# Softmax of a gated attention layer on one core: eight of sixteen heads shifted and exponentiated by ScalarE instead of VectorE

## What is computed

```
q = LN(x) Wq + bq;  k = ctx Wk + bk;  v = ctx Wv + bv     (16 heads of width 64)
probs = softmax(q k^T / 8)                                (over the 64 context rows, for each head)
x = x + tanh(g_xattn) * (probs v Wo + bo)
x = x + tanh(g_ffn) * FFN(LN(x))        (a shared expert, and the best 2 of 8 experts for each token)
```

## Time and profile before

| | us |
|---|---|
| median of 3 runs | 307.4 |
| lowest and highest | 306.29, 309.32 |
| the profiled execution's own time | 309.48 |
| its span, first to last instruction | 307.7 |
| PE busy, share of the span | 278.0, 90% |
| DVE busy | 241.7, 79% |
| ACT busy | 163.9, 53% |
| POOL busy | 170.0, 55% |

### The profile page before, as it was taken

The page is one execution under the profiler, slowest core; times in us unless marked ns, Lnnn a source line. Parts: engine busy times, 40 slices in busy tenths (PEclk is TensorE's granted clock), DMA queues, the critical chain, the costliest instruction groups (busy, mean ns, idle before and its releaser), DMA issues.

```text
span 307.7 us, 6608 instructions
## 1 busy us (share of the span) xinstructions
PE 278.0 (90%) x1746; PEld 248.8 (81%) x1747; DVE 241.7 (79%) x687; ACT 163.9 (53%) x426; POOL 170.0 (55%) x236
## 2 busy tenths in 40 slices
PE   2999979999999899999986969987799999999992
PEld 1788757898897798999876948876799899999881
DVE  0489869999999699989999575778877777777755
ACT  1462785666756566673653434744355565657611
POOL 8012216787757876897886775409553444444520
PEclk9999999999999999999998897999999999999999
DMA  6999994133379999713031122313244434343697
GB/s 186 367 295 318 269 293 119 47 90 94 102 207 292 306 315 325 223 36 105 35 104 37 53 87 88 90 53 105 69 123 126 118 92 121 113 129 105 223 344 264
DMA packets 45006, 49.74 MB, mean 162 GB/s; under 512 B 3928, under 2 KB 41650, under 8 KB 44978
## 3 DMA queue, kind: packets, MB, share of 16 engines
q1 hardware_dynamic: 39938, 39.37, 44.4%
q0 software_dynamic: 3408, 8.46, 8.1%
q10 hardware_dynamic: 1632, 1.57, 1.5%
HBM read 21.67 MB, written 28.64 MB: 163 GB/s over the span
## 4 chain that ended last, share of the span: by engine, by line
PE 47%; DVE 26%; issue 9%; DMA 6%; ACT 6%; POOL 3%; SPq 1%; DVEq 0%; ACTq 0%; POOLq 0%
PE bank L1404 5%; PE bank L1406 4%; PE bank L1405 4%; PE scores_ps L1404 4%; DVE probs L1156 4%; PE scores_ps L1406 3%; DVE pT_lo L1133 3%; DVE row_sum L1140 3%; PE scores_ps L1405 3%; PE bank L1350 3%; DMA Wk_sb<-in_L_xattn_Wk_dram 3%; DMA AB_free<-routed_dram 2%; DVE row_max L1150 2%; PE bank L1601 2%; PE scores_ps L1441 2%
## 5 line engine op out<-in xcount | busy, mean ns | idle before, releaser
L691 POOL DMA_INDIRECT routed_dram<-probs,sct_idx x39 | 38.0, 975 | 57.1 <-ACT probs L915 55.6
L648 POOL TENSOR_TENSOR probs<-probs,row_inv 128x1024 f32<-128x1024 f32 x16 | 30.5, 1908 | 25.2 <-DVE row_inv L1144 24.9
L612 POOL DMA_INDIRECT rows_dram<-xn,slot_i x32 | 32.0, 1001 | 14.6 <-issue 11.2
L1404 PE MATMUL bank<-AB_hi,pT_hi 128*128 128x256 f32 x128 | 37.7, 294 | 2.2 <-DVE pT_lo L1133 2.2
L1406 PE MATMUL bank<-AB_hi,pT_lo 128*128 128x256 f32 x128 | 36.5, 285 | 0.0
L1405 PE MATMUL bank<-AB_lo,pT_hi 128*128 128x256 f32 x128 | 36.4, 285 | 0.0
L771 ACT ACTIVATE probs<-probs 128x1024 f32<-128x1024 f32 x16 | 16.9, 1058 | 29.6 <-DVE probs L1156 29.6
L1404 PE MATMUL scores_ps<-AB_hi,xnT_hi 128*128 128x512 f32 x64 | 26.4, 413 | 1.8 <-DVE xnT_lo L1126 1.7
L1404 PEld LDWEIGHTS bank<-AB_hi,pT_hi 128*128 128x128 f32 x128 | 24.9, 194 | 2.7 <-issue 2.5
L1406 PE MATMUL scores_ps<-AB_hi,xnT_lo 128*128 128x512 f32 x64 | 25.3, 396 | 0.0
L1405 PE MATMUL scores_ps<-AB_lo,xnT_hi 128*128 128x512 f32 x64 | 25.3, 395 | 0.0
(11 more groups left out here) (249 smaller groups left out, 886.4 us busy)
## 6 DMA issues: line engine op xcount, KB each, us to landing
rows_dram<-pad_rows SPq DMA_DIRECT2D x10, 1040.0 KB, 15.8
rows_dram<-pad_rows SPq DMA_DIRECT2D x8, 780.0 KB, 12.5
AB_free<-routed_dram SPq DMA_DIRECT2D x8, 512.0 KB, 7.9
probs<-rows_dram SPq DMA_DIRECT2D x30, 130.0 KB
raw_buf<-in_L_ffn_Wg_dram SPq DMA_DIRECT2D x8, 192.0 KB, 2.5
raw_buf<-in_L_ffn_Wu_dram SPq DMA_DIRECT2D x8, 192.0 KB, 2.9
out_dram<-x_sb ACTq DMA_DIRECT2D x6, 256.0 KB, 2.7
pT_hi<-rows_dram SPq DMA_DIRECT2D x9, 130.0 KB
```

Of the source, the lines that this page charges most:

```text
L612: nc.gpsimd.indirect_dma_start(rows_dram[:, :], bass.IndirectOffsetOnAxis(ap=slot_i[:, t, k:k + 1], axis=0), xn2[:, t % KEEP, :], None).th ...
L648: nc.gpsimd.tensor_tensor(pr, pr, row_inv[:, :].unsqueeze(2).to_broadcast([P, H, KV]), ALU.mult).then_inc(norm_done, 1)
L691: nc.gpsimd.indirect_dma_start(routed_dram[:, :], bass.IndirectOffsetOnAxis(ap=sct_idx[(k - 2) % (2 * RING)][:, 0:1], axis=0), y_sb[ks][:, ...
L1404: nc.tensor.matmul(out_ap, a_hi, b_hi, start=first, stop=False)
```

## The change

The second eight heads (the second bank of `scores_ps`) no longer pass through the subtraction. ACT reads `row_max` after `max_rows`, writes its negative for these heads into a small new tile `neg_max`, and then runs eight exponentials of 128 x 64, one for each head, straight from `scores_ps` into `prob`, with the head's column of `neg_max` as per-partition bias (the new function `shifted_exponentials`). The subtraction on DVE and the exponential on ACT shrink to the first eight heads, 128 x 512 each. PE waits ahead of the second half of `scores` for `shifted_done`, DVE's `max_rows` for `neg_max_done`, and `sum_rows` for `shifted_done` besides `exp_done`.

```diff
+        neg_max = sb("neg_max", [P, H // 2])
...
-                nc.scalar.activation(prob[m % 2][:, :], prob[m % 2][:, :], ACT.Exp).then_inc(exp_done, 1)
+                nc.scalar.activation(prob[m % 2][:, 0:HK // 2], prob[m % 2][:, 0:HK // 2], ACT.Exp).then_inc(exp_done, 1)
+
+            def shifted_exponentials(u):
+
+                act.wait_ge(max_done, u + 1)
+                after(act, pT_done, 2 * u - 2)
+                nc.scalar.activation(neg_max[:, :], row_max[:, H // 2:], ACT.Copy, scale=-1.0).then_inc(neg_max_done, 1)
+                act.wait_ge(neg_max_done, u + 1)
+                for h in range(H // 2, H):
+                    last = nc.scalar.activation(prob[u % 2][:, h * KV:(h + 1) * KV], scores_ps[:, h * KV:(h + 1) * KV], ACT.Exp,
+                                                bias=neg_max[:, h - H // 2:h - H // 2 + 1])
+                last.then_inc(shifted_done, 1)
...
             B_high([0])
+            shifted_exponentials(0)
             exponentials(0)
...
-            B_high([2, 3])
+            B_high([2])
+            shifted_exponentials(1)
+            B_high([3])
             exponentials(1)
...
             shared_high()
+            shifted_exponentials(2)
...
                     round_down((TB, TB + 2, TB + 5).index(t))
+                if inside(u):
+                    shifted_exponentials(u)
...
                 dve.wait_ge(exp_done, m + 1)
+                dve.wait_ge(shifted_done, m + 1)
...
                 after(dve, sub_done, u)
+                after(dve, neg_max_done, u)
                 nc.vector.tensor_reduce(row_max[:, :], by_head, AX_X, ALU.max).then_inc(max_done, 1)
...
-                nc.vector.tensor_tensor(prob[u % 2][:, :].rearrange("p (h k) -> p h k", k=KV), by_head,
-                                        row_max[:, :].unsqueeze(2).to_broadcast([P, H, KV]),
+                nc.vector.tensor_tensor(prob[u % 2][:, 0:HK // 2].rearrange("p (h k) -> p h k", k=KV), by_head[:, 0:H // 2, :],
+                                        row_max[:, 0:H // 2].unsqueeze(2).to_broadcast([P, H // 2, KV]),
                                         ALU.subtract).then_inc(sub_done, 1)
...
                 for half in range(2):
+                    if half:
+                        after(pe, shifted_done, u)
```

More of the change, by code:

```diff
@@ L312, in flamingo_layer @@
         exp_done = sem("exp_done")
+        neg_max_done = sem("neg_max_done")
+        shifted_done = sem("shifted_done")
         sum_done = sem("sum_done")
```

## The result

| | before | after |
|---|---|---|
| median in the same comparison, us (12 runs each) | 308.55 | 310.67 |
| lowest and highest | 306.29, 309.47 | 308.94, 313.72 |
| profiled execution, own time and span | 309.48, 307.7 | 309.88, 308.1 |
| DVE busy | 241.7 | 233.4 |
| ACT busy | 163.9 | 186.0 |

The ratio is 1.0079 with a 95% interval of 1.0055 to 1.0104: the change costs 2.1 us (1.7 to 3.2), 0.8%. That is clear of no difference at all, but under the 1% that the forecast calls no change. The forecast was +0.9%.

What follows compares the result with a forecast made beforehand. Bound by the softmax chain through ACT, PE nearly as tight. Prologue 1.9 + step 4 0.6 + link 0.3 - end 0.1 = +2.7 us: 310.1 on the 307.4 median (312.2 on the profiled execution), range 306.5 to 315.

Steps and rivals of the forecast that it cites:

- the prologue: Tiles 0 to 2, ahead of the loop: the new blocks on ACT hand +1.9 us to the loop.
- step 4: Loop step where two roundings on ACT outlast the maximum, so the new block starts late: +0.6 us.
- The link: Loop step, end of the maximum to `high_x`: 2.49 us instead of 2.46, +0.3 us over about ten steps.
- Nearest row, only shorter: Small exponentials on ACT, priced from L715 with 192 fewer columns: 0.21 us each, eight make 1.68.
- The mild rival: Small exponentials on ACT overlap by 0.07 instead of 0.10: 0.24 us each, 313.0 us in all; chance 0.13.
- the one without overlap: Each small exponential on ACT waits out the one before: 0.33 us each, +12 on the forecast, 322; chance 0.10.
- the free bias: Repeated bias column costs nothing on ACT: 0.10 us an exponential, block 0.88 shorter, 302.5 us; chance 0.09.
- Step 10: Loop step given no lateness term of its own; ACT was said mostly to idle at the end of its step.
- The end: Tile 15, ending with the same link: the shorter subtraction takes off perhaps 0.1 us.
- The waits: PE's new wait in `scores`: free in the loop, maybe half a us in tile 1, covered; `max_rows` never held.
- PE's clock in the prologue: PE's clock drops there because the change adds waiting for ACT and DVE: 1.5 us lost, 311.6; chance 0.13.

Runs made afterwards that it cites:

- one bias: Kernel after the change, but eight heads share head 8's negated maximum, one 128 x 512 exponential replacing eight; 305.04 us, ratio 0.9892 to the kernel before.
- sixteen halves: Kernel after the change, each small exponential split into two of 32 columns, sixteen instead of eight; 327.77 us, ratio 1.0643 to the kernel before.

## Why the prediction was right, step by step

- **The time.** +2.7 us on the profiled execution, +0.9%, was forecast; the comparisons give +2.1 us, 0.79% and 0.74%, and the interval of 1.7 to 3.2 us holds both. The profiled execution itself was put at 312.2 and took 309.88: its span is 0.4 longer than before, of which -1.2 lies ahead of the first `low_x`, +2.6 from there to tile 15, and -1.0 behind it; the first and the last vary by themselves from one execution to the next. The main terms held: the prologue and step 4, and a loop that neither gains nor loses in the other steps.
- **The link** was put at 2.49 for 2.46, +0.3 us over ten steps. It was 2.38, and to the end of `high_x` 2.81 for 2.82: the term is 0. The exponentials stand 0.198 apart (0.21 taken from L715 of the earlier trace rows), the copy with its wait takes 0.25 (0.22), the halved exponential 0.52 (0.55). "Nearest row, only shorter" was good to 6%, in part by luck: its working makes a record 0.47 - 0.16 = 0.31 long with an overlap of 0.10, and measured are 0.329 and 0.131, two misses that offset each other. The mild rival, 0.24, and the one without overlap, 0.33, are refuted, and so is the free bias, 0.10. That last rival's price for a link 0.88 shorter, -4.9 us (302.5 for 307.4), was too high as well: one bias has the shorter link and gained 3.3, because PE holds the loop sooner than the prediction took it to.
- **The Trainium skill**, "ScalarE: Activation LUTs" (what ACT_TABLE_LOAD costs), gives by its figures 0.333 us for one of 64 columns, an estimate; the group of L783 has 0.329 on average, which agrees. Its overlap of about 93 ns does not agree: 0.329 - 0.198 = 0.131. By that page of the Trainium skill the exponentials would stand 0.24 apart, an estimate; the trace decides, and the time is not the 313.0 of that rival.
- **The prologue**: +1.9 forecast, 1.75 measured, and 0.38% when it was changed alone. By blocks: 1.48 and 1.4 forecast for tiles 1 and 2, 1.45 and 1.31 measured. The rest is the shorter block, 0.25 + 1.58 = 1.83 for 1.90.
- **Step 4**: +0.6 forecast, the shift grows by 0.58.
- **Step 10**: missed, 0.17. The prediction judged the other steps by step 8 alone, where ACT idled. The rounding of step 8 does fit, with 0.59 to spare; the one of step 10 holds the copy until 0.22 after the maximum, for 0.03 elsewhere. In step 3 one costs 0.03 more.
- **The end**: -0.1 forecast; tile 15 ends with what the loop had, 2.57, so the term is not seen. The 0.8 missing behind the loop goes with one wait of 1.36 us in the one trace of the kernel before. Why the sum of +2.7 and the shift of 2.6 lie above the median difference of +2.1 stays open; all three lie within the interval.
- **The waits** came out as said: PE waits for L783 once, 0.4 us ahead of the scores of tile 1 in the prologue (half a us was put down, covered), never in the loop, and `max_rows` never waits for the copy.
- **PE's clock in the prologue**: it does drop in some executions, of the change in the prologue alone and of the whole change. It did not in the profiled one. The rival put the price at 1.5 us, taken from a stretch behind the loop. There a drop does cost 1.0 to 1.2; in the prologue it costs less than 0.1, so this rival had its price wrong, and not only its chance.

## What to carry to other kernels

Relieving a busy engine gains nothing where its work lay beside another engine's: follow the distance between the two ends of the link, here from the maximum to the end of `high_x`, and price the new instructions one by one on the engine that the link runs through. Splitting one instruction into eight for the sake of a bias column costs eight times a price of which about three quarters does not depend on the columns; one shift for all heads keeps the benefit (no subtraction) without it. And before an instruction is moved off the link, look who waits for it: `low_xn2`, 1.1 to 1.3 us later, cost PE as much as the shorter link gave. Where another engine is nearly tied with the link, a longer link costs in full and a shorter one gains little.

## What the runs showed that was not expected

The small exponentials leave something behind on ACT. Within a block the records of the eight grow from 0.306 to as much as 0.358 us, though they start 0.198 apart, and the instructions behind them show longer records until ACT next idles. The groups of the kernel after (mean ns behind the bar) against 594 for `high_p` and 369 for `high_x` (L754, of the kernel before, the last line):

```profile
L783 ACT ACTIVATE probs<-scores_ps,neg_max 128x64 f32<-128x64 f32 x128 | 27.9, 329 | 0.5
L793 ACT ACTIVATE pT_hi<-bank 128x512 fp32r<-128x512 f32 x32 | 18.2, 653 | 1.0 <-PE bank L1525 1.0
L757 ACT ACTIVATE xnT_hi<-bank 128x256 fp32r<-128x256 f32 x16 | 6.8, 423 | 5.5 <-PE bank L1517 5.4
L754 ACT ACTIVATE xnT_hi<-bank 128x256 fp32r<-128x256 f32 x16 | 5.9, 369 | 8.8 <-PE bank L1495 8.7
```

With sixteen halves `high_x` takes 0.50, and with one exponential of 128 x 512 or 128 x 1024 in their place it is back at 0.38 and `high_p` at 0.596. So the end of an instruction falls behind its start while many small ones run, by 0.06 us for eight and 0.13 for sixteen, and who waits for a later one on the same engine pays it. What in the engine does this isn't shown.

An exponential of 128 x 1024 with a bias, read from both banks of PSUM, holds ACT's queue for 1.01 us (117.49 to 118.50), that of before from SBUF for 0.97: the bias and the other source together cost 0.04 here.
